# A two-layer attention network and a graph convolution on one core: the last layer is moved into both sides of a runtime branch, its bias goes from GpSimd to VectorE, and the steps around it are laid out anew

## The reference, cut to what matters

```python
def _gat_layer(h, adj, W, b):                 # twice, N = 4096 nodes, 128 features
    A = softmax(where(adj > 0, h @ h.T / sqrt(128), NEG), axis=1)
    A = A * 0.5;  A[d, d] += 0.5
    A = where(mask[:, None], 0.0, A);  A[d, d] = where(mask, 1.0, A[d, d])
    return relu(A @ (h @ W.T + b))

def _L1_gnn_ref(x, adj, W, b):                # the last layer
    a_hat = adj + eye(N);  s = sum(a_hat, axis=1) ** -0.5
    return ((a_hat * s[:, None] * s[None, :]) @ x) @ W.T + b

h = maximum(layernorm(x), 0);  x = x + two _gat_layers(h)
h = maximum(layernorm(x), 0);  x = x + _L1_gnn_ref(h, adj, ...)
```

## Time and profile before

| | |
|---|---|
| median of the runs | 1009.04 us (1003.52 to 1010.0) |
| the profiled execution | 1005.73 us |
| its span in the trace | 1003.9 us |
| mean granted TensorE clock | 0.988 |
| busy: TensorE, VectorE, ScalarE, GpSimd | 960.1, 540.2, 444.2, 82.3 us |
| the chain that ended last, TensorE's share | 92% |

### The profile page before, as it was taken

The page is one execution under the profiler, slowest core; times in us unless marked ns, Lnnn a source line. Parts: engine busy times, 40 slices in busy tenths (PEclk is TensorE's granted clock), DMA queues, the critical chain, the costliest instruction groups (busy, mean ns, idle before and its releaser), DMA issues.

```text
span 1003.9 us, 16182 instructions
## 1 busy us (share of the span) xinstructions
PE 960.1 (96%) x6598; PEld 872.5 (87%) x6598; DVE 540.2 (54%) x962; ACT 444.2 (44%) x641; POOL 82.3 (8%) x75
## 2 busy tenths in 40 slices
PE   3999999999999999998999999999999998699998
PEld 2899999999999999988999999999999997577776
DVE  3555444454545453545554765755666777734443
ACT  3655666666666666621111221222121222475564
POOL 3761000000000000005000000000000000400000
PEclk9899999999999999999999999999999999889999
DMA  9976888888989988750000000000000001300000
GB/s 240 217 168 171 196 235 207 218 214 224 212 216 212 220 215 223 189 173 2 1 1 12 11 2 11 12 1 12 11 12 12 14 19 42 101 0 32 11 22 22
DMA packets 101968, 103.26 MB, mean 103 GB/s; under 512 B 72960, under 2 KB 79872, under 8 KB 101888
## 3 DMA queue, kind: packets, MB, share of 16 engines
q1 hardware_dynamic: 101376, 101.94, 40.4%
q0 software_dynamic: 80, 0.02, 0.1%
q10 hardware_dynamic: 432, 0.20, 0.1%
HBM read 77.48 MB, written 7.86 MB: 85 GB/s over the span
## 4 chain that ended last, share of the span: by engine, by line
PE 92%; DVE 3%; DMA 2%; ACT 1%; issue 1%; SPq 1%; DVEq 0%; ACTq 0%
PE pAcc L1120 36%; PE pMisc L1187 10%; PE pS L1039 9%; PE pS L1037 9%; PE pS L1038 9%; PE pS L1267 6%; PE pS L1268 5%; PE pTurn L1174 5%; DMA adjT<-nat 1%; PE pMisc L1253 1%; DMA x_scratch<-x_block 1%; DVE x_block L812 1%; ACT adj_wide L602 1%; DVE prob L919 0%; ACT aggT L608 0%
## 5 line engine op out<-in xcount | busy, mean ns | idle before, releaser
L1120 PE MATMUL pAcc<-feat,prob 128*128 128x129 f32 x3200 | 393.8, 276 | 9.1 <-DVE prob L898 6.9
L1120 PEld LDWEIGHTS pAcc<-feat,prob 128*128 128x128 f32 x3200 | 382.6, 192 | 22.7 <-DVE prob L898 7.3
L898 DVE TENSOR_TENSOR prob<-prob,adjT 128x1024 f32<-128x1024 f32 x128 | 156.8, 1225 | 202.8 <-ACT prob L550 195.9
L570 ACT ACTIVATE prob<-pS 128x1024 f32<-128x1024 f32 x72 | 73.7, 1024 | 308.9 <-PE pTurn L1174 273.3
L550 ACT ACTIVATE prob<-pS 128x1024 f32<-128x1024 f32 x128 | 130.9, 1022 | 140.8 <-PE pS L1039 140.8
L1037 PE MATMUL pS<-high 128*128 128x512 f32 x400 | 174.6, 436 | 0.0
L1039 PE MATMUL pS<-high,low 128*128 128x512 f32 x400 | 158.6, 396 | 0.0
L1038 PE MATMUL pS<-low,high 128*128 128x512 f32 x400 | 156.6, 391 | 0.0
L506 ACT ACTIVATE nat<-chunk 128x1024 uint8<-128x1024 f32 x128 | 134.4, 1050 | 13.8 <-DMA adjT<-nat 11.6
L1267 PE MATMUL pS<-adj_wide,z_high 128*128 128x512 f32 x256 | 106.7, 417 | 17.8 <-DVE adj_wide L1010 9.3
L1187 PE MATMUL pMisc<-feat,turned_prob 128*128 128x129 f32 x896 | 118.4, 275 | 0.0
(11 more groups left out here) (119 smaller groups left out, 550.7 us busy)
## 6 DMA issues: line engine op xcount, KB each, us to landing
chunk<-in_adj_dram SPq DMA_DIRECT2D x128, 512.0 KB, 4.5
x_in<-in_x_dram SPq DMA_DIRECT2D x8, 256.0 KB, 6.2
adjT<-nat SPq DMA_TRANSPOSE x128, 3.4
x_block<-in_x_dram SPq DMA_DIRECT2D x8, 256.0 KB, 2.8
x_scratch<-x_block SPq DMA_DIRECT2D x8, 256.0 KB, 2.0
x<-x_scratch SPq DMA_DIRECT2D x8, 256.0 KB, 4.7
hiT_scratch<-highT SPq DMA_DIRECT2D x7, 256.0 KB, 5.0
loT_scratch<-lowT SPq DMA_DIRECT2D x7, 256.0 KB, 4.9
```

The costliest lines, as they stand in the source:

```text
L898: nc.vector.tensor_tensor(pr, pr, adj_unit(b, u), ALU.mult).then_inc(prob_ready[L], 1)
L1120: mm = nc.tensor.matmul(pAcc[:, t // 2, (t % 2) * W:(t % 2 + 1) * W], prob[:, buf, h, t * P:(t + 1) * P], feat[:, 2 * u + h, :], start=(fi ...
```

## The change

- The last layer becomes a function on ScalarE, VectorE and TensorE (`last_layer`, with `aggregate` and `project` on TensorE) that is called at the end of both sides of the branch. SP's end (loads of x1, stores of the result) stays behind it; its loads of x for blocks 6 and 7, of the bias, and its store of block 6's x1 go into both sides. GpSimd's roots of blocks 6 and 7 also go inside.
- Tiles k = 0 and 1 (`SOON`) are multiplied ahead of the last unit's mix. ScalarE and VectorE enter the last layer when A of block 6 is done (`acc_kept[1] >= 7`), not when the last unit is.
- A new step S (`biased`) on VectorE writes x1 plus the bias into `mixed`, for each block. SP stores that. GpSimd's eight additions are dropped. G no longer waits for the store; A of the next block and `keep_agg` do.
- D is only the statistics now, and L the self loops. `post_at` and `TAIL` are laid out anew.

The tables, and the rest of the diff cut to its core:

```diff
-        TAIL = {2: ((6, "RD"),), 5: ((7, "A"), (6, "E")), 8: ((7, "B"),), 11: ((6, "FG"),), 14: ((7, "CR"),), 17: ((6, "H"),),
-                20: ((7, "D"),), 23: ((7, "E"),), 29: ((7, "FG"),), 35: ((7, "H"),)}
-        TAIL_HIGH = {13: 6, 31: 7}
+        TAIL = {2: ((6, "D"),), 5: ((6, "E"),), 8: ((7, "A"), (6, "F")), 11: ((6, "G"),), 14: ((7, "B"),), 17: ((6, "H"), (7, "C")),
+                20: ((7, "RS"),), 23: ((7, "D"),), 26: ((7, "E"),), 29: ((7, "F"),), 32: ((7, "G"),), 38: ((7, "H"),),
+                44: ((6, "L"),), 47: ((7, "L"),)}
+        TAIL_HIGH = {13: 6, 34: 7}
+
+        SOON = 2
...
             if n >= 8:
-                return {0: "A", 1: "B", 2: "CR", 3: "D", 4: "E", 6: "FG", 7: "H"}.get(v, "")
-            return {6: ("A", "B", "CR", "DE", "FG", "H"), 4: ("A", "BCR", "DE", "FG"), 2: ("A", "BC")}[n][v]
+                return {0: "A", 1: "B", 2: "CR", 3: "SD", 4: "LE", 6: "FG", 7: "H"}.get(v, "")
+            return {6: ("A", "B", "CRS", "DLE", "FG", "H"), 4: ("A", "BCR", "SDLE", "FG"), 2: ("A", "BCRS")}[n][v]
...
+            def store_x1(b):
+                sp.wait_ge(x1_biased, b + 1)
+                sp.dma_start(x1_dram[:, RT * b:RT * (b + 1), :], mixed[:, :, 0:E]).then_inc(x1_stored, 16)
+
+            def load_bias():
+                sp.wait_ge(tiny_ready[1], 1)
+                sp.dma_start(bg_all[:, :], bg.rearrange("(a d) -> a d", a=1).broadcast_to([P, P])).then_inc(bg_loaded, 16)
 
             def symmetric():
+                load_bias()
                 for b in range(LEFT):
                     sp.wait_ge(exp_ready[1], ROW_END[b])
                     load_x(b, x_block[:, b, :, :])
-                    store_x1(b, x_block[:, b, :, :])
-                sp.wait_ge(exp_ready[1], len(SEQ))
+                    store_x1(b)
+                for b in range(LEFT, NB):
+                    sp.wait_ge(exp_ready[1], ROW_END[b])
+                    load_x(b, x_block[:, b, :, :])
+                    if b == LEFT:
+                        store_x1(b)
 
...
             second_attention(sp, symmetric, guarded)
-            for b in range(LEFT, NB):
-                load_x(b, x_block[:, b, :, :])
-            sp.wait_ge(tiny_ready[1], 1)
-            sp.dma_start(bg_all[:, :], bg.rearrange("(a d) -> a d", a=1).broadcast_to([P, P])).then_inc(bg_loaded, 16)
-            sp.wait_ge(adj_used, 1)
+            sp.wait_ge(adj_used, SOON + 1)
             sp.wait_ge(z_low_ready, LEFT)
             for b in range(NB):
-                if b >= LEFT:
-                    store_x1(b, x_block[:, b, :, :])
+                if b == NB - 1:
+                    store_x1(b)
                 sp.wait_ge(x1_stored, 16 * (b + 1))
...
             second_attention(pool, plain, guarded)
-            for b in range(LEFT, NB):
-                root_x1(b)
-
-            pool.wait_ge(bg_loaded, 16)
-            for b in range(NB):
-                pool.wait_ge(x1_loaded[b], 16)
-                rows = x1[:, RT * b:RT * (b + 1), :]
-                nc.gpsimd.tensor_tensor(rows, rows, bg_all[:, :].rearrange("p (a d) -> p a d", a=1).broadcast_to([P, RT, P]),
-                                        ALU.add).then_inc(x1_biased, 1)
 
...
+                act.wait_ge(acc_kept[1], NB - 1)
+                last_layer()
 
...
+                act.wait_ge(x1_stored, 16 * NB)
...
+            second_attention(act, symmetric, guarded)
...
-                    wait(dve, x1_made, b)
+                    wait(dve, x1_stored, 16 * b)
...
+            def biased(b, x_rows_b):
+
+                dve.wait_ge(x1_made, b + 1)
+                dve.wait_ge(bg_loaded, 16)
+                nc.vector.tensor_tensor(mixed[:, :, 0:E], x_rows_b,
+                                        bg_all[:, :].rearrange("p (a d) -> p a d", a=1).broadcast_to([P, RT, P]),
+                                        ALU.add).then_inc(x1_biased, 1)
...
-                dve.wait_ge(x1_stored, 16 * (b + 1))
...
                     residual(b, rows)
+                if "S" in letters:
+                    biased(b, rows)
                 if "D" in letters:
                     statistics(b, rows)
+                if "L" in letters:
                     add_self_loops(b)
...
+                dve.wait_ge(acc_kept[1], NB - 1)
+                last_layer(len(SEQ))
 
...
-                dve.wait_ge(x1_biased, b + 1)
+                dve.wait_ge(x1_loaded[b], 16)
...
+            def last_layer(units):
+                for k in range(NB * NJ):
+                    if not wide_on_act(k):
+                        widen(k)
+                    if k in TAIL:
+                        for b, letters in TAIL[k]:
+                            if "A" in letters:
+                                dve.wait_ge(prob_used[1], units)
+                            post(b, letters)
+                    if after_block(k, 7) is not None:
+                        finish(after_block(k, 7))
+                finish(NB - 1, range(0, RT // 2))
+                finish(NB - 1, range(RT // 2, RT))
+
+            second_attention(dve, symmetric, guarded)
...
+
+            def aggregate(k):
+                b, t = AGG[k]
+                by_act, by_dve = wide_before(k)
+                if wide_on_act(k):
+                    pe.wait_ge(wide_by_act, by_act + 1)
+                else:
+                    pe.wait_ge(wide_by_dve, by_dve + 1)
+                if b == 0 and t % RT == 0:
+                    pe.wait_ge(z_low_ready, t // RT + 1)
+                if t == 0:
+                    wait(pe, agg_kept, b - 3)
+                nc.tensor.matmul(agg_bank(b), z_high[:, t, :], slot(k), start=(t == 0), stop=False)
+                nc.tensor.matmul(agg_bank(b), z_low[:, t, :], slot(k), start=False,
+                                 stop=(t == NJ - 1)).then_inc(adj_used, 1)
+
+            def last_layer(begin):
+                for k in range(begin, NB * NJ):
+                    aggregate(k)
+                    if after_block(k, 4) is not None:
+                        project(after_block(k, 4))
+                project(NB - 1, range(0, RT // 2))
+                project(NB - 1, range(RT // 2, RT))
...
+                    if g == len(SEQ) - 1:
+                        for k in range(SOON):
+                            aggregate(k)
                     mix(1, b, u, 1, g, 2 * b)
...
                 pe.wait_ge(exp_ready[1], len(SEQ))
+                last_layer(SOON)
```

More of the change, by code:

```diff
@@ L448, in plain @@
                 totals()
-                for b in range(LEFT):
+                for b in range(NB):
                     root_x1(b)
@@ L470, in guarded @@
                         root_x1(b)
+                for b in range(LEFT, NB):
+                    root_x1(b)
             for grp in range(4):
@@ L1190, in mix_turned, with project @@
                 mm.then_inc(turned_used, 1)
+            def project(b, tiles=range(RT)):
+                pe.wait_ge(agg_kept, b + 1 + (b == NB - 1 and tiles[0] > 0))
+                wait(pe, res_ready, b)
+                for t in tiles:
+                    mm = nc.tensor.matmul(project_bank(b, t)[:, t * P:(t + 1) * P], aggT[:, t * P:(t + 1) * P], WgT[:, :],
+                                          start=True, stop=True)
+                mm.then_inc(res_made, 1)
+            def aggregate(k):
+                b, t = AGG[k]
+                by_act, by_dve = wide_before(k)
+                if wide_on_act(k):
+                    pe.wait_ge(wide_by_act, by_act + 1)
[15 more added lines that the diff above has]
+                project(NB - 1, range(RT // 2, RT))
             def symmetric():
```

71 lines of the change are left out of this document (19 added, 52 removed).

## The result

| | before | after |
|---|---|---|
| median of the runs shared with before | 1006.28 us (1001.4 to 1010.0, 4 runs) | 990.13 us (988.96 to 996.3, 4 runs) |
| the profiled execution | 1005.73 us | 988.96 us |
| its span | 1003.9 us | 987.1 us |
| mean granted TensorE clock | 0.988 | 0.994 |

The ratio of after to before is 0.9875, with a 95% interval of 0.9836 to 0.9914. On 1006.28 us that is a gain of 12.6 us (8.7 to 16.5); the two profiled executions differ by 16.8, and the medians by 16.2. Some executions of either kernel lie 7 to 9 us above its fastest: 1009.04 and 1010.0 before, 996.3 after.

What follows compares the result with a forecast made beforehand. TensorE's stops and half clock in the last sixth were taken as the bound, 19.5 us lost before tile 79. Gain 17.8, less 1.0 at the end, is 16.8: from 1009.04 to 992 us, range 986 to 1000.

Steps and rivals of the forecast that it cites:

- T1: Stretch from the end of the attention's last mix to the end of tile k = 79; forecast 39.1 us.
- The three causes: TensorE's stops behind the last mix: branch jump, G waiting for block 6's store, GpSimd's bias adds; 12.7 us in all.
- The stop of 2.0 us: Behind the last mix, TensorE's stop shrinks from 3.38 to 2.0 us, until VectorE's copy of tile 2.
- The full clock behind it: After the shortened stop behind the last mix, TensorE's granted clock stays at 1.00.
- the first two cases: Behind the last mix: full clock kept, 992 us (0.55), or clock falls in the 2 us stop, 994 (0.22).
- the second case: Rival: the clock falls in the 2 us stop behind the last mix; +2.2 us, 994; chance 0.22.
- Pacing 0.7: From tile 2 to tile 23, VectorE's steps and copies make it 0.7 us late; bounds 0 to 2.
- Two tiles ahead: Tiles 0 and 1, 0.93 us, fit TensorE's 1.39 us wait before its last mix and cost nothing; 78 tiles remain.
- The store lands in 2.0 us: Block 6's x1 store, issued ahead of all x1 loads, lands in 2.0 us; A of block 7 doesn't wait.
- G at 1.1 us, six S hidden: G of block 7 takes about 1.1 us without GpSimd's adds; six S of 0.69 in the attention cost nothing.
- The end at +1.0: At the program's end, each engine takes the branch's jump behind its last work; +1.0 us, bounds 0 to 1.4.
- the rival with the late store: A of block 7 waits for a store taking 6.64 us; +5.2 us, 997; chance 0.12.

Runs made afterwards that it cites:

- before_short: The kernel before with the guarded side of the branch left empty, so the jump over it is short; 1002.58 us, T1 52.34.
- the join: The kernel before with only the last layer moved into both sides of the branch; bias, stores and loads as before; 1002.16 us, T1 53.07.
- soon0: The changed kernel without the two tiles ahead of the last mix; 989.9 us, T1 38.70 for 80 tiles.
- early: The changed kernel with VectorE's copies of tiles 2 and 5 ahead of B of block 6; 988.85 us, ratio to before 0.9838, T1 39.17.
- d_later_soon0: As d_later, without the two tiles ahead of the last mix; 989.02 us, ratio to before 0.9845, T1 37.35 for 80 tiles.
- d_later: As early, with TAIL's steps spread one to a copy and D, E, A, F, G each behind one more copy; 985.36 us, ratio to before 0.9824.
- pool_bias: The changed kernel with the bias added by GpSimd again, no S, and G waiting for the store; 996.27 us, T1 45.23.

## Why the prediction was right, and where it was not

The forecast span, 987.1, is the measured one, and 990.13 against 992 lies inside the range. But the sum came out through errors that cancel, which is luck: T1 is 1.1 longer than forecast, the end 0.2 cheaper, and the last mix lies 1.0 earlier, which no part of the change made. That 1.0 is there before the branch into the second attention layer, ahead of the code that differs: ScalarE comes to that branch at 457.5 instead of 458.5 us, and the stop before it ends at 454.09 instead of 455.11.

- **The three causes: right.** The jump and GpSimd's additions were taken out of the kernel before one at a time, and the store's place was put back in the changed kernel. The jump: 4.5 us of T1 (before_short), 3.8 by the join. GpSimd's additions: 9.1 alone, 5.0 inside the changed kernel. The store's place: 8.3 when put back. They don't add up to the 16.65 that the change brought; they were measured in different kernels, and one wait hides part of another, as the 0.97 us in before_short show.
- **The stop of 2.0 us, ended by VectorE's copy of tile 2: right** (2.01).
- **The full clock behind it: wrong.** This was the choice between the first two cases, 0.55 against 0.22, and it rested on two rows. One was the 2.4 us at 452.7 in a single execution; the same stop lost the clock in 6 of 13 profiles. The other was the 1.00 through the stop of 860.0 to 863.1, but the row behind it reads 0.52, so that stop did lose the clock, only behind its end, as the one of 2.01 us did here. The half clock costs 0.11 + 1.55, with what lies behind 852.20 1.7 us. So the second case happened, and the sign that the prediction had set for itself, a clock of 0.5 after the stop, came up. Its price was too high: forecast 2.85 of half clock less 0.7 of pacing, +2.2; measured 1.73 less the 0.7 that did not come, +1.1.
- **Pacing 0.7: 0 here, 0.35 at the full clock.** TensorE has no wait for a copy behind 848.29 in after; at half clock it leaves VectorE the room. soon0 has the same table and the full clock behind its stop, and shows 0.35 us, inside the bounds of 0 to 2. The 2.7 us of early are no measure of this term, since there VectorE has no stop to catch up in.
- **Two tiles ahead "cost nothing": mis-sized.** I looked at the gap they fill and not at the stop behind the mix, which they lengthen by a wait for someone else. soon0 shows 1.5 us: 1.0 of stop and 1.7 of half clock less, 0.9 of tiles and 0.35 of pacing more.
- **The store lands in 2.0 us: nearly.** 2.2 was the shortest of the new stores. VectorE was ready for A of block 7 at 850.07, 1.0 earlier than forecast, and started it at 850.39, 2.55 behind the start of the store's issue. So VectorE did idle before A, the second of the prediction's own signs, but by 0.32 us, which cost TensorE nothing. The Trainium skill (DMA: Bandwidth & Descriptors, Specifications) had runs of 512 B at the full rate; 2.2 against 2.0 us agrees.
- **G at 1.1 us, six S hidden: right.** TensorE is busy throughout the attention as before, and from the end of the stop at 452 to the last mix the same 392.2 us pass.
- **The end at +1.0: the size nearly right (0.8), the path not.** The prediction had TensorE arrive 1.4 late by a branch of 5.05 us or VectorE 0.8 late, and SP's last event later than the last store explains. TensorE's branch took 3.39 us. SP's last event comes 0.4 us behind the end of its wait for the last store, with the jump and without it, and it is that store that is slower.
- **The price of the rival with the late store: too small**, 5.2 against 8.3, since the loads ahead of the store wait too, and the half clock lasts longer behind the longer stop.
- **The median.** I took the profiled execution's distance of 3.3 us to the median over to the changed kernel. But the runs of before fall into two groups, 1000 to 1004 us at a mean clock of 0.989 to 0.995, and 1007 to 1010 at 0.981 to 0.986, most likely by the stop at 452 (only one execution that is so far above its kernel's fastest has a profile, that of d_later_soon0), and 1009.04 was of the second. The changed kernel has one such execution as well, 996.3 us at 0.986. For the gain the ratio's 12.6 us are a better figure than the 16.8 of one pair. Why the profiled execution of before, which kept the clock at 452, lies 4 us above the fastest beside it (1001.4) is not settled.

## What to carry to other kernels

Work put into a gap ahead of a stop is worth something only if it is TensorE that is late behind it: follow the stop to the engine that ends it, and move that engine's instruction (here two copies) first. A stop costs its length and, often, the clock behind it, so closing small stops can bring more than their idle time: from after to d_later T1 fell by 3.7 us, to 36.47 of a possible 36.4, and only 2.0 of them had been idle. A row of one profile says what the clock did once; where the runs of a kernel fall into two groups, look in profiles of both for the stop behind which the clock differs. And when an edit's price comes out right, check the path too: here the end cost about what was forecast, by a store that stood nowhere in the sum.

## What the runs showed of the hardware

- **The clock behind a stop.** All stops of TensorE of 0.9 us or more from 440 to 470 and from 838 to 912 us, in all fourteen profiles, by the granted clock in the eight us behind each:

| stop of TensorE | seen | clock fell to 0.50 behind it |
|---|---|---|
| 0.94 to 1.39 us | 11, two of them followed by a stop of over 3 us | none of the other 9 |
| 1.94 to 2.02 us | 4 | 4 |
| 2.38 us at 452 | 13 | 6 |
| 2.41 to 6.2 us | 10 | 10 |

- A stop of 2.38 us thus kept the clock more often than one of 2.0 us. The place may count, or what TensorE did before, or it is chance (at 6 in 13, four losses in a row come in 5 of 100 cases); which is open. The fall comes up to 1.6 us behind the end of the stop (0.6 in after), and the half clock lasts 3 to over 15 us.
- **A far jump** stalls TensorE 5.05 or 3.39 us, VectorE 2.8 or 3.3, ScalarE 2.8; with the other side empty TensorE's branch takes 0.33. For VectorE and ScalarE it doesn't show in the branch's own duration, only in the time to the next instruction.
- **A store beside far jumps:** the issue of the last output store took 0.78 to 1.21 us in the ten profiles where the engines jump far at the end, and 0.34 in the other four.
- **GpSimd beside VectorE:** in pool_bias instructions of 0.16 to 0.43 us take 1.2 to 1.5 each beside additions of 1.29; one copy of 0.41 was spared.
